# TensorE's order in a group pass: the sums over spans in two blocks behind up 7 and down 5, and up of chunk 0 ahead of routing

## The chip, the core and the metric

The kernel runs on one core of a Trainium2 chip. The core has TensorE (matmuls), VectorE (DVE), ScalarE (ACT), GpSimd (POOL) and SyncE (SP, which here starts DMAs), each with its own instruction stream; they meet only at semaphores. The metric is the time of one execution in microseconds (us), the median over several runs.

## What is computed

A block of a network over 16 sequences of 256 tokens with 128 features, in fp32: a selective-scan layer (a state-space recurrence with 16 states), and behind it a feed-forward layer with one shared expert and eight routed ones, of which each token takes two. Both are modulated by a small table of scales and shifts. Cut to what matters:

```python
h = _layernorm(x) * (1 + ca) + sa
xc, z = split(h @ W_in)
xs = silu(conv(xc) + conv_b)                     # 4 taps along time
x_dbl = xs @ W_x
delta = softplus(x_dbl[..., :1]); Bp = ...; Cp = ...
A_bar = exp(delta * A); B_bar = delta * Bp
h_t = A_bar_t * h_(t-1) + B_bar_t * x_t;  y_t = sum_n h_t * C_t
x = x + ga * (((y + D * xs) * silu(z)) @ W_out)
h = _layernorm(x) * (1 + cb) + sb
out = swiglu(h, shared) + sum over top 2 of 8 experts: weight * swiglu(h, expert)
x = x + gb * out
```

The kernel doesn't step through time. It multiplies by decays exp(a * sum of delta over a span), for spans that halve (128, 64, 32, 16) and for pairs of tokens within blocks of 16. The sums of delta over these spans are matmuls of constant 0/1 matrices with delta: these are the "sums over spans".

## The kernel before

The 4096 tokens are worked in eight groups of 512 (two sequences). The loop over groups is `body(g, prev, head)`, written once for each engine: body(0) outside a loop, body(1) to body(6) in a hardware loop, body(7) behind it. In a pass three pieces of work are woven together, each engine's order written out by hand:

- the head of group g+1 (`head`): layer norm, W_in (project_in), convolution, W_x (project_x), softplus, the sums over spans, the decays and factors;
- the middle of group g: factors turned (turn_factors), weighed and mixed (weigh, mix), W_out (project_out), residual, second norm, h2 turned (turn_h2);
- the tail of group g-1 (`prev`): routing logits and picks, and the shared expert in eight chunks c of its 938 hidden features. Each chunk has `gate(c)` and `up(c)`, three 512-column matmuls each (a weight's low part, high part, and the input's low part), a silu on ScalarE, a product on VectorE, a split into high and low parts (`ah`, `al`), and `down(c)`, which adds to one result bank. The numbers "up 7", "down 5" and "product 6" mean these chunks. Chunk 3 is the short one.

In the passes ("NARROW") all gates share PSUM bank 5 and all ups bank 6, so gate(c) waits until silu c-1 has read the bank, and up(c) until product c-1 has. The tail's result is copied by ScalarE (y_sb), turned by TensorE (turn_result), multiplied on VectorE into `gated`, and added to X on GpSimd.

The sums over spans (`sum_spans(g+1)`, line 722) wait for `delta_ready`, which VectorE gives with dl_upto (line 1290), and end with `spans_done`, for which VectorE's `level_exponents` (line 1293 and on) waits. They are five products with delta (ten matmul records of 2 or 4 columns: fp32 takes two passes) and one with dl_upto (two records, 64 columns). In VectorE's order stand make_delta (delta, dl_upto, dB), product 6, second_norm (nx_b, h2), product 7, level_exponents, pair_exponents, low_x, factors, gate_shared (gated), pairs_by_c, take_logits; then in the next body product 0, sum_pairs (wd, line 1341), product 1. GpSimd's pairs_by_b (pair, line 489) stands between pairs_by_c and sum_pairs.

`route(g-1)` is twelve matmuls of 8 columns that wait for xh and xl, the high and low parts of the tail's input; turn_x waits for nx_a, ScalarE's normalised input of the next head.

Behind the passes stands the wide part: the last group's shared expert and the routed experts' tiles, and then the final sum.

Of the kernel before, what the change touches and what calls it, by code (L numbers as in the profile page):

```python
# [39 lines left out]
GC = CH // G  # L40
# [73 lines left out]
def adaln_block(nc, a):  # L114
    ctx = ExitStack()
    with ctx:
        def sb(name, shape, dt=F32):
            return ctx.enter_context(nc.sbuf_tensor(name, shape, dt))

        def sem(name):  # L120
            return ctx.enter_context(nc.semaphore(name))
# [8 lines left out]
        M = {n: mats[:, i, :] for i, n in enumerate(CONST)}  # L130
# [43 lines left out]
        delta = sb("delta", [P, GC])  # L174
# [58 lines left out]
        PS = ctx.enter_context(nc.psum_tensor("PS", [P, 8, 512], F32))  # L233
# [4 lines left out]
        NARROW = {"gate": (5,), "up": (6,), "down": 7, "turn": 5}  # L238
# [6 lines left out]
        def bank(kind, where, c=0):  # L245
            b = where[kind]
            return PS[:, b if isinstance(b, int) else b[c % len(b)], :]

        def part_of(c):

            return c if c < SHORT else FC - 1 if c == SHORT else c - 1
# [21 lines left out]
        s = {n: sem("s_" + n) for n in names}  # L273
# [327 lines left out]
        def _(pe):  # L601
            def mm(out, lhsT, rhs, start=True, stop=True, **k):
                return nc.tensor.matmul(out, lhsT, rhs, start=start, stop=stop, **k)  # L603

            def turn(out, src):
                return nc.tensor.transpose(out, src, M["ident"])  # L606

            def high_part(out, buf, w0, rh, start):

                mm(out, w_lo[buf][:, w0:w0 + P], rh, start, False)  # L610
                mm(out, w_hi[buf][:, w0:w0 + P], rh, False, False)

            def low_part(out, buf, w0, rl, stop):

                return mm(out, w_hi[buf][:, w0:w0 + P], rl, False, stop)
# [15 lines left out]
            def up(buf, I, c, where):  # L631
                out = bank("up", where, c)
                if where is NARROW and c:
                    pe.wait_ge(s["prod_done"], I * FC + c)
                w0 = UP + part_of(c) * P
                high_part(out, buf, w0, xh[:], True)
                low_part(out, buf, w0, xl[:], True).then_inc(s["up_done"], 1)
# [6 lines left out]
            def down(buf, I, c, where):  # L644
                pe.wait_ge(s["ah_ready"], I * FC + c + 1)
                out, w0 = bank("down", where), DOWN + part_of(c) * P
                if c != SHORT:
                    high_part(out, buf, w0, ah[:, c % 3, :], c == 0)
                else:
                    mm(out, w_lo[buf][0:FL, w0:w0 + P], ah[0:FL, c % 3, :], False, False)  # L650
                if where is WIDE:
                    pe.wait_ge(s["al_ready"], I * FC + c + 1 - (FC - CUT) * (G - 1))
                elif c < CUT:
                    pe.wait_ge(s["al_ready"], I * CUT + c + 1)
                else:
                    pe.wait_ge(s["al_late"], I * (FC - CUT) + c - CUT + 1)
                if c != SHORT:
                    last = low_part(out, buf, w0, al[:, c % 3, :], c == FC - 1)
                else:
                    last = mm(out, w_hi[buf][0:HALF + FL, w0:w0 + P], ah[0:HALF + FL, c % 3, :], False, False)  # L660
                if c == FC - 1:
                    last.then_inc(s["y_bank_done"], 1)
                elif c < FC - 3:
                    last.then_inc(s["down_done"], 1)
# [49 lines left out]
            def gather_c(g):  # L714

                pe.wait_ge(s["cexp_ready"], g + 1)
                pe.wait_ge(s["xst_ready"], 2 * g + 2)
                for k in range(2):
                    mm(PS[:, 3 + k, :], M["upto16"], c_exp[:, 2 * k:2 * k + 2].rearrange("p j a n -> p (j a n)")
                       ).then_inc(s["cg_done"], 1)  # L720

            def sum_spans(g):

                pe.wait_ge(s["delta_ready"], g + 1)
                out = PS[:, 2, 256:256 + 4 * GC].rearrange("p (l j) -> p l j", l=4)
                mm(out[:, 0, 0::2], M["below7"], delta[:, 0::2])
                mm(out[:, 0, 1::2], M["above7"], delta[:, 1::2])
                for k, n in enumerate(("lvl6", "lvl5", "lvl4")):
                    mm(out[:, k + 1, :], M[n], delta[:])
                mm(PS[:, 2, 320:320 + GC * BLK], M["later16"], dl_upto[:].rearrange("p j a -> p (j a)")).then_inc(  # L730
                    s["spans_done"], 1)

# [39 lines left out]
            def turn_h2(g, more):  # L772
                pe.wait_ge(s["h2_ready"], g + 1)
                if more:
                    pe.wait_ge(s["sz_ready"], 2 * g + 4)
                for j in range(GC):
                    last = turn(PS[:, 0, j * P:(j + 1) * P], h2[:, 0, j, 0:P])
                last.then_inc(s["h2T_done"], 1)

            def route(g):  # L780
                pe.wait_ge(s["xh_ready"], g + 1)
                pe.wait_ge(s["xl_ready"], g + 1)
                for j in range(GC):
                    o = PS[:, 1, j * E:(j + 1) * E]
                    mm(o, xl[:, j * P:(j + 1) * P], gate_hi[:], True, False)
                    mm(o, xh[:, j * P:(j + 1) * P], gate_lo[:], False, False)
                    last = mm(o, xh[:, j * P:(j + 1) * P], gate_hi[:], False, True)
                last.then_inc(s["logits_done"], 1)
# [19 lines left out]
            project_x(0)  # L808
            turn_xs(0, True)
            sum_spans(0)  # L810
            gather_c(0)

            def body(g, prev, head):
                if prev:
                    route(g - 1)
                if head:
                    turn_x(g + 1, False, prev)
                if prev:
                    gate(0, g - 1, 0, NARROW)
                    up(0, g - 1, 0, NARROW)  # L820
                    gate(0, g - 1, 1, NARROW)
                    up(0, g - 1, 1, NARROW)
                turn_factors(g)
                if prev:
                    gate(0, g - 1, 2, NARROW)
                if head:
                    project_in(g + 1, 0, prev)
                weigh(g)
                if prev:
                    up(0, g - 1, 2, NARROW)  # L830
                    count_picks(g - 1, COUNTS)
                    up(0, g - 1, 3, NARROW)
                mix(g, 0)
                if prev:
                    gate(0, g - 1, 4, NARROW)
                if head:
                    project_in(g + 1, 1, prev)
                mix(g, 1)
                if prev:
                    gate(0, g - 1, 5, NARROW)  # L840
                if head:
                    project_in(g + 1, 2, prev)
                if prev:
                    down(0, g - 1, 0, NARROW)
                if head:
                    project_in(g + 1, 3, prev)
                if prev:
                    up(0, g - 1, 4, NARROW)
                    gate(0, g - 1, 6, NARROW)
                project_out(g, head)  # L850
                if prev:
                    gate(0, g - 1, 7, NARROW)
                    down(0, g - 1, 1, NARROW)
                    up(0, g - 1, 5, NARROW)
                if head:
                    project_x(g + 1)
                if prev:
                    down(0, g - 1, 2, NARROW)
                if head:
                    turn_xs(g + 1, False)  # L860
                if prev:
                    down(0, g - 1, 3, NARROW)
                    down(0, g - 1, 4, NARROW)
                    up(0, g - 1, 6, NARROW)
                if head:
                    sum_spans(g + 1)
                if prev:
                    up(0, g - 1, 7, NARROW)
                    down(0, g - 1, 5, NARROW)
                turn_h2(g, head)  # L870
                if head:
                    gather_c(g + 1)
                if prev:
                    down(0, g - 1, 6, NARROW)
                    down(0, g - 1, 7, NARROW)
                    turn_result(g - 1, NARROW)

            body(0, False, True)
            pe.wait_ge(s["split_done"], 1)
            apart(pe)  # L880
# [813 lines left out]
```

## Time and profile before

| | |
|---|---|
| Time, median of 3 runs | 783.69 us (783.38 to 783.82) |
| The profiled execution's own time | 781.73 us |
| Its span, first to last instruction | 779.9 us |
| TensorE busy | 669.7 us, 86% of the span |
| VectorE busy | 561.2 us, 72% |
| ScalarE busy | 431.6 us, 55% |
| GpSimd busy | 375.4 us, 48% |
| Mean granted TensorE clock | 0.928 of full speed |

The profile is of one execution. Its times count from the span's start. A timeline lists the instructions of one engine: start, duration, line, operation, out<-in, shape, how many were merged, and in brackets the idle time ahead of it and what ended that. Line 603 is the helper `mm` and 606 the helper `turn` of TensorE, 1248 the product, 961 the silu. Ends of matmuls are modelled: from the start of one to the start of the next is the surer price. A granted clock of 1.00 is 2.4 GHz, 0.50 is 1.2 GHz.

### The profile page before, as it was taken

To read this page: it belongs to the slowest core of one execution; us is meant where nothing else is said; L and a number is where in the kernel's file an instruction comes from. 1 tells how busy PE (TensorE), PEld (TensorE's weight loads), DVE (VectorE), ACT (ScalarE), POOL (GpSimd) and SP (SyncE) were. 2 spreads that over 40 slices of the span, in tenths; PEclk is the share of its full clock that TensorE was granted. 3 is DMA by queue.
4 is the path that set the end of the run, shared out by engine and by line. 5 is a ranking of instruction groups with operands and counts; after the bars stand their busy time and mean duration, and the time that the engine had idled before them with its cause. 6 is when DMAs were issued, how large, how long until landed. Compare 5 with 4: busy or idle time off the path is not lost.

```text
span 779.9 us, 12016 instructions
## 1 busy us (share of the span) xinstructions
PE 669.7 (86%) x3026; PEld 503.3 (65%) x3027; DVE 561.2 (72%) x1230; ACT 431.6 (55%) x822; POOL 375.4 (48%) x299
## 2 busy tenths in 40 slices
PE   4768989899899989897789998999999998999910
PEld 1546767677666766674557776777677776777700
DVE  4878969889797979985647665666666675766637
ACT  4457566675757656653445554555555565555600
POOL 1323654647384554636318291836154172922145
PEclk9598979999998989989799999999999999999965
DMA  8303000000000000010310322313103103110046
GB/s 257 90 1 96 28 27 19 10 30 24 27 27 27 27 12 28 14 34 22 116 49 6 128 65 82 92 41 116 39 17 116 41 4 116 43 34 21 27 139 194
DMA packets 41297, 44.55 MB, mean 57 GB/s; under 512 B 8052, under 2 KB 31976, under 8 KB 41280
## 3 DMA queue, kind: packets, MB, share of 16 engines
q1 hardware_dynamic: 36672, 35.88, 15.6%
q0 software_dynamic: 4608, 8.47, 3.3%
q8 instruction: 7, 0.11, 0.1%
q14 instruction: 10, 0.08, 0.0%
HBM read 31.61 MB, written 13.76 MB: 58 GB/s over the span
## 4 chain that ended last, share of the span: by engine, by line
PE 37%; DVE 27%; issue 16%; POOL 11%; DMA 3%; SPq 2%; ACT 2%; POOLq 1%; DVEq 1%; ACTq 0%
PE PS L603 33%; POOL w_lo L434 4%; PE PS L606 4%; DVE acc L1268 3%; POOL w_hi L429 3%; DVE al L1255 3%; DVE prod L1248 2%; SPq L306 2%; DMA xin<-sorted_dram 1%; POOL pair L489 1%; DVE yT L1358 1%; DVE wd L1341 1%; POOL result_dram L562 1%; DVE PS L1248 1%; POOL sorted_dram L499 1%
## 5 line engine op out<-in xcount | busy, mean ns | idle before, releaser
L961 ACT ACTIVATE sg<-PS 128x512 f32<-128x512 f32 x216 | 128.7, 596 | 150.1 <-PE PS L603 148.8
L603 PE MATMUL PS<-xh,w_lo 128*128 128x512 f32 x405 | 177.2, 438 | 15.8 <-issue 7.1
L1248 DVE TENSOR_TENSOR PS<-PS,sg 128x512 f32<-128x512 f32 (+1 forms) x160 | 111.3, 697 | 109.1 <-PE PS L603 98.3
L562 POOL DMA_INDIRECT result_dram<-y_rows,aux_d x80 | 78.0, 975 | 186.7 <-DVE y_rows L1620 156.1
L603 PE MATMUL PS<-xh,w_hi 128*128 128x512 f32 x405 | 162.9, 402 | 0.0
L603 PE MATMUL PS<-xl,w_hi 128*128 128x512 f32 x405 | 162.8, 402 | 0.0
L499 POOL DMA_INDIRECT sorted_dram<-h,slot x64 | 74.0, 1156 | 90.0 <-DVE slot L1455 64.1
L603 PEld LDWEIGHTS PS<-xh,w_lo 128*128 128x128 f32 x405 | 78.3, 193 | 48.8 <-DVE prod L1248 13.5
L1255 DVE TENSOR_TENSOR al<-PS,ah 128x512 fp32r<-128x512 f32 x140 | 95.5, 682 | 7.7 <-ACT ah L969 5.0
L603 PE MATMUL PS<-ah,w_lo 128*128 128x512 f32 x216 | 96.5, 447 | 3.8 <-ACT ah L969 3.8
L969 ACT CAST ah<-PS 128x512 fp32r<-128x512 f32 (+1 forms) x160 | 92.8, 580 | 8.5 <-DVE PS L1248 8.1
L603 PEld LDWEIGHTS PS<-xl,w_hi 128*128 128x128 f32 x405 | 78.7, 194 | 18.2
L603 PE MATMUL PS<-ah,w_hi 128*128 128x512 f32 x216 | 88.6, 410 | 0.8 <-DVE ah L1255 0.8
L603 PEld LDWEIGHTS PS<-xh,w_hi 128*128 128x128 f32 x405 | 78.9, 195 | 13.4 <-issue 1.4
L603 PE MATMUL PS<-al,w_hi 128*128 128x512 f32 x189 | 76.0, 402 | 2.3 <-POOL al L452 1.2
L603 PEld LDWEIGHTS PS<-ah,w_lo 128*128 128x128 f32 x216 | 41.2, 191 | 22.6 <-issue 11.2
L1248 DVE TENSOR_TENSOR prod<-PS,sg 128x512 f32<-128x512 f32 (+1 forms) x56 | 38.5, 688 | 20.1 <-PE PS L603 14.1
L603 PEld LDWEIGHTS PS<-ah,w_hi 128*128 128x128 f32 x216 | 41.6, 192 | 16.8 <-issue 8.0
L969 ACT CAST ah<-prod 128x512 fp32r<-128x512 f32 (+1 forms) x56 | 34.4, 615 | 32.5 <-DVE prod L1248 29.8
L452 POOL TENSOR_TENSOR al<-prod,ah 128x512 fp32r<-128x512 f32 x28 | 38.7, 1384 | 20.5 <-ACT ah L969 20.4
L434 POOL TENSOR_TENSOR w_lo<-stage,w_hi 128x3072 fp32r<-128x3072 f32 x7 | 47.9, 6838 | 0.6
L603 PEld LDWEIGHTS PS<-al,w_hi 128*128 128x128 f32 x189 | 36.2, 191 | 12.9 <-DVE al L1255 3.1
(223 smaller groups left out, 1114.9 us busy)
## 6 DMA issues: line engine op xcount, KB each, us to landing
stage<-in_w_gu SPq DMA_DIRECT2D x18, 448.0 KB
xin<-sorted_dram SPq DMA_DIRECT2D x20, 260.0 KB, 2.7
stage<-in_w_dn SPq DMA_DIRECT2D x9, 448.0 KB
tab<-mods_dram SPq DMA_DIRECT2D x8, 384.0 KB, 3.6
sorted_dram<-pad SPq DMA_DIRECT2D x8, 260.0 KB, 2.4
out<-X SPq DMA_DIRECT2D x4, 512.0 KB, 3.2
stage<-result_dram SPq DMA_DIRECT2D x3, 512.0 KB, 5.2
result_dram<-y_rows,aux_d POOLq DMA_INDIRECT x80, 2.2
```

Of the source, the lines that this page charges most:

```text
L429: V.tensor_tensor(w_hi[buf][:], stage[:], M["ones"][:, 0:1].to_broadcast([P, WC]), ALU.mult).then_inc(s["split_hi"], 1)
L434: V.tensor_tensor(w_lo[buf][:], stage[:], w_hi[buf][:].bitcast(F32), ALU.subtract).then_inc(s["split_done"], 1)
L452: V.tensor_tensor(al[:, c % 3, :], prod[:, c % 3, :], ah[:, c % 3, :].bitcast(F32), ALU.subtract).then_inc(s["al_late"], 1)
L499: pool.indirect_dma_start(out=sorted_dram, out_offset=bass.IndirectOffsetOnAxis(ap=slot[:, k, j:j + 1].bitcast(U32), axis=0), in_=h2[:, k, ...
L562: pool.indirect_dma_start(out=result_dram, out_offset=bass.IndirectOffsetOnAxis(ap=aux_d[:, r:r + 1].bitcast(U32), axis=0), in_=y_rows[:, ...
L603: return nc.tensor.matmul(out, lhsT, rhs, start=start, stop=stop, **k)
L606: return nc.tensor.transpose(out, src, M["ident"])
L961: A.activation(dst, src, ACT.Silu).then_inc(s["silu_done"], 1)
L969: A.copy(ah[0:n, c % 3, :], product_in(where, c)[0:n, :]).then_inc(s["ah_ready"], 1)
L1248: V.tensor_tensor(product_in(where, c)[0:n, :], bank("up", where, c)[0:n, :], sg[0:n, c % 3, :], ALU.mult).then_inc(s["prod_done"], 1)
L1255: V.tensor_tensor(dst, product_in(where, c)[0:n, :], ah[0:n, c % 3, :].bitcast(F32), ALU.subtract).then_inc(s["al_ready"], 1)
L1268: last = V.scalar_tensor_tensor(o, xcp[:, h, :, k:k + SEQ], cols[:, h, k:k + 1], o, ALU.mult, ALU.add)
```

## The change

TensorE's stream alone is changed, in three places. (1) `sum_spans` keeps the sums with below7, above7 and lvl6; the rest (lvl5, lvl4 and the one on dl_upto, with the increment of `spans_done`) is a new function, `sum_low_spans`. (2) In body, sum_spans(g+1) stands behind up 7 instead of ahead of it, and sum_low_spans(g+1) behind down 5. (3) up(0) of the tail stands ahead of route, behind waits for xh and xl, instead of behind gate(0).

```diff
@@ sum_spans
                 mm(out[:, 0, 1::2], M["above7"], delta[:, 1::2])
-                for k, n in enumerate(("lvl6", "lvl5", "lvl4")):
-                    mm(out[:, k + 1, :], M[n], delta[:])
+                mm(out[:, 1, :], M["lvl6"], delta[:])
+
+            def sum_low_spans(g):
+
+                out = PS[:, 2, 256:256 + 4 * GC].rearrange("p (l j) -> p l j", l=4)
+                for k, n in ((2, "lvl5"), (3, "lvl4")):
+                    mm(out[:, k, :], M[n], delta[:])
                 mm(PS[:, 2, 320:320 + GC * BLK], M["later16"], dl_upto[:].rearrange("p j a -> p (j a)")).then_inc(
                     s["spans_done"], 1)
@@ before the loop
             sum_spans(0)
+            sum_low_spans(0)
             gather_c(0)
@@ body
                 if prev:
+                    pe.wait_ge(s["xh_ready"], g)
+                    pe.wait_ge(s["xl_ready"], g)
+                    up(0, g - 1, 0, NARROW)
                     route(g - 1)
                 if head:
                     turn_x(g + 1, False, prev)
                 if prev:
                     gate(0, g - 1, 0, NARROW)
-                    up(0, g - 1, 0, NARROW)
                     gate(0, g - 1, 1, NARROW)
                     up(0, g - 1, 1, NARROW)
...
                     up(0, g - 1, 6, NARROW)
+                if prev:
+                    up(0, g - 1, 7, NARROW)
                 if head:
                     sum_spans(g + 1)
                 if prev:
-                    up(0, g - 1, 7, NARROW)
                     down(0, g - 1, 5, NARROW)
+                if head:
+                    sum_low_spans(g + 1)
                 turn_h2(g, head)
```

## Rows read from the trace of the kernel before

**Rows 1.** The page, part 4: the chain's shares of the span by engine.
```profile
PE 37%; DVE 27%; issue 16%; POOL 11%; DMA 3%; SPq 2%; ACT 2%; POOLq 1%; DVEq 1%; ACTq 0%
```

**Rows 2.** Chain that ended last, in pass 5: start us, us, what, count.
```profile
277.62 5.12 PE PS L603 x18
...
287.44 0.59 ACT y_sb L973
...
288.94 0.70 DVE gated L1462
...
292.32 1.30 POOL pair L489
```

**Rows 3.** TensorE's timeline, pass 5: start, us, line, operation, [idle before].
```profile
277.62 1.92 PE L603 MATMUL PS<-delta,mats 128*128 128x2 f32 x10 [1.12 <-DVE dl_upto L1290]
...
279.83 0.78 PE L603 MATMUL PS<-xh,w_lo 128*128 128x512 f32 x1
...
281.26 0.63 PE L603 MATMUL PS<-ah,w_lo 128*128 128x512 f32 x1
...
282.54 1.05 PE L606 MATMUL PS<-mats,h 128*128 128x128 f32 x4
...
285.46 0.79 PE L603 MATMUL PS<-ah,w_lo 128*128 128x512 f32 x1
```

**Rows 4.** VectorE's timeline, pass 5.
```profile
277.49 1.30 DVE L1292 TENSOR_TENSOR dB<-delta,dbc 128x64 f32<-128x64 f32 x1
279.07 0.69 DVE L1248 TENSOR_TENSOR prod<-PS,sg 128x512 f32<-128x512 f32 x1 [0.28 <-DVE dB L1292]
...
282.16 0.41 DVE L1297 TENSOR_TENSOR lev<-PS,a_neg 128x256 f32<-128x256 f32 x1
...
286.67 0.75 DVE L1324 TENSOR_TENSOR pq<-lev_b,small 128x64 f32<-128x64 f32 x3
```

**Rows 5.** Windows: us, busy by engine, granted clock, DMA share, GB/s; pass 5.
```profile
279.00:280.00 1.00, 1.00 (x6) 1.00 (x7) 0.93 (x2) 0.14 (x1) 0.00 (x0) 0.50 0.00 0
285.00:286.00 1.00, 1.00 (x4) 0.52 (x3) 0.96 (x6) 0.65 (x2) 0.00 (x0) 1.00 0.00 0
```

**Rows 6.** Pass 6: TensorE's timeline, VectorE's, and one window.
```profile
322.12 1.28 PE L603 MATMUL PS<-delta,mats 128*128 128x2 f32 x10 [1.12 <-DVE dl_upto L1290]
323.26 0.41 PE L603 MATMUL PS<-dl_upto,mats 128*128 128x64 f32 x2
324.31 0.50 PE L603 MATMUL PS<-xh,w_lo 128*128 128x512 f32 x1 [0.64 <-DVE prod L1248]
...
329.17 0.40 PE L603 MATMUL PS<-al,w_hi 128*128 128x512 f32 x1
...
331.18 0.68 DVE L1462 TENSOR_TENSOR gated<-PS,tab_g 128x512 f32<-128x512 f32 x1
...
325.00:326.00 1.00, 1.00 (x7) 0.65 (x6) 0.68 (x1) 0.96 (x2) 0.94 (x1) 1.00 0.00 0
```

**Rows 7.** Pass 1: VectorE's timeline, then TensorE's.
```profile
101.42 0.69 DVE L1248 TENSOR_TENSOR prod<-PS,sg 128x512 f32<-128x512 f32 x1 [0.28 <-DVE dB L1292]
...
103.63 0.77 PE L603 MATMUL PS<-xh,w_lo 128*128 128x512 f32 x1
```

**Rows 8.** Tile dl_upto: duration ns min/median/max of its weight loads.
```profile
L603 PEld LDWEIGHTS PS<-dl_upto,mats x16: 192/333/333, 29.3 to 323.3; 128*128 128x128 f32 x16
```

**Rows 9.** Around up 0 and gate 1, pass 5: TensorE, then VectorE, then ScalarE.
```profile
290.33 0.63 PE L606 MATMUL PS<-mats,nx_a 128*128 128x128 f32 x4 [0.21 <-ACT nx_a L1053]
...
291.49 0.40 PE L603 MATMUL PS<-xh,w_lo 128*128 128x512 f32 x1
...
292.34 0.50 PE L603 MATMUL PS<-xh,w_lo 128*128 128x512 f32 x1
...
292.45 0.69 DVE L1248 TENSOR_TENSOR prod<-PS,sg 128x512 f32<-128x512 f32 x1 [1.18 <-PE PS L603]
...
291.68 0.60 ACT L961 ACTIVATE sg<-PS 128x512 f32<-128x512 f32 x1 [0.29 <-PE PS L603]
```

## The prediction

> **What bounds the kernel now.** I read the page first, and of it the chain of work that ended last: it lies 37% on TensorE and 27% on VectorE [rows 1]. A share over 780 us mixes stages, so next comes the chain in order of time inside one group pass. The changed order acts in body(g) for g = 1 to 7, of which passes 1 to 6 also hold the head of the next group, and so the sums over spans. They repeat every 44.5 us; I work on pass 5 (the one whose end lies near 287 us) and hold it against passes 1 and 6. There the chain is short to tell: from the sums over spans at 277.62 TensorE runs without a stop, over up 7, down 5, the turn of h2, the gathering of C, down 6 and down 7, to the copy of the result at 287.44. Behind it stand ScalarE's copy y_sb, the turn of the result, VectorE's gated at 288.94, GpSimd's pair product up to 293.62, and then the reduction to wd, from which VectorE's routing of the tail goes on [rows 2]. So from 277.62 to 287.4 TensorE is the bound of the pass, and its orders there count one for one.
>
> Then I ask what starts that stretch. In TensorE's rows up 6 ends about 276.5, the engine stands 1.12 us until dl_upto is written, the 12 records of the sums start at 277.62, and up 7 at 279.83 [rows 3]. In VectorE's rows dB runs from 277.49 to 278.79 and product 6, which up 7 must wait for (one PSUM bank serves all "up" chunks of a narrow pass), from 279.07 to 279.76 [rows 4]. Up 7 thus starts 0.07 us behind product 6: the sums lie in a hole that up 7 could not have used. That is the observation on which the forecast rests.
>
> **The change part by part.**
>
> *Sums over spans, moved behind up 7 and down 5.* The work is the same: 12 records in all. At the old place they fill the hole 277.6 to 279.8; at the new one the hole stays empty, and they stand inside the stretch where TensorE is the bound. Their price, start to next start: 279.83 - 277.62 = 2.21 us at half speed [rows 3]; at full speed 323.26 - 322.12 = 1.14 for the ten narrow ones and 0.41 for the two on dl_upto, 1.55 us [rows 6].
>
> What they gain: up 7 may start when product 6 ends. In pass 5 that is 279.76 against 279.83, so nothing; in pass 6 up 7 already stands behind product 6 (0.64 us of idle, released by it) [rows 6]. Only pass 1 has a gain: its product 6 ends at 102.11, up 7 starts at 103.63 [rows 7], 1.5 us, of one pass.
>
> What could hide them: a wait of TensorE behind up 7. Down 5 at 281.26, the turn of h2 at 282.54 and down 6 at 285.46 all start with no idle ahead of them [rows 3], and the chain stays on TensorE up to y_sb [rows 2]. There is none.
>
> Who waits for the later sums: level_exponents on VectorE, queued behind product 7, with the pair exponents, low_x, the factors and gated behind it. The sums would be done at 279.83 + 1.43 (up 7) + 1.28 (down 5) + 2.21 = 284.75. From the start of the exponents at 282.16 to the end of the factors at 287.42 VectorE takes 5.26 us, of which some is a wait for xh; from 284.75 that gives 290.0 [rows 4]. Gated needs the result's turn, so it moves from 288.94 [rows 2] to about 291. So VectorE stays ahead by 0.8 to 1 us and adds nothing at half speed. ScalarE (level and pair exponentials) follows VectorE's exponents and comes before y_sb in its queue; y_sb waits for down 7, some 2 us later than now, so this adds nothing either. No DMA, no queue of SP or GpSimd is passed; GpSimd only waits for gated, later.
>
> *The clock.* In pass 5 the granted clock is 0.50 (1.2 of 2.4 GHz) in 279:280, and 1.00 again in 285:286 [rows 5]. Before the fall the engine had stood 1.12 us and then run only narrow sums. In pass 6 it stayed at 1.00 behind the same idle time [rows 6]. Over all passes the weight loads for dl_upto took 192 ns at least and 333 ns in the median [rows 8], so at least half of the 16 ran slowly. After the change TensorE stands from 276.5 to 279.8, 3.3 us instead of 1.1, and the narrow sums then lie between wide matmuls. I expect the low level in all six passes, and for at least as long as now. Price of this, with pass 5's own durations: up 7 1.43, sums 2.21, down 5 1.28, turn and gathering 282.54 to 285.46, 2.92, downs 6 and 7 285.46 to about 287.4, 1.95 [rows 2, 3]; 9.8 us from up 7's start to the last down, against 7.6 now. In pass 6, all at full speed, it is 324.31 to 329.57, 5.3 us now [rows 6], so there up to +4.5. If the downs too run slowly (six at 0.43, from 281.26 to 282.54 for three) the stretch has 10.4 us.
>
> The sum: for passes 1 to 5 the added time lies between the sums' full-speed price 1.55 and their half-speed price 2.21. I take 2.0, since the granted clock has usually come back for the last downs and pass 1 gives some of it back. For pass 6, which loses the full clock, I take 4.0 of the 4.5. 5 x 2.0 + 4.0 = 14.0 us.
>
> *Up of chunk 0 ahead of routing.* Three wide matmuls, 292.34 less 291.49, 0.85 us, move ahead of the 12 routing matmuls. Nobody waits for them sooner: product 0 starts at 292.45 behind up 0, but the reduction behind it is bound by GpSimd's pair product, which ends at 293.62 and starts when it is done with gated [rows 2, 9]. The hole that takes them is small: the turn of x starts at 290.33 when nx_a is there, behind 0.21 us of idle. So the turn, gate 0 and silu 0 come about 0.45 us later (0.6 to 0.7 of up 0 less the idle), silu 0 at 292.1 for 0.60; product 0 no longer waits for up 0 at 292.45 but for silu 0 near 292.75, and ends at 293.45 instead of 293.14, still ahead of 293.62. The logits come some 0.7 us later, and their copy has an idle stretch of 1.18 us behind it on VectorE [rows 9]. Cost 0; bounds from the hole's 0.2 us gained and 0.3 us lost (product 0's shift, if the pair product came earlier), times 7: -1.4 to +2.1. In pass 7, without a turn of x, gate 0 and the rest shift by the same and end in the same wait.
>
> *Setup.* sum_spans(0) and sum_low_spans(0) stand together, and body(0) has nothing between them: no change. Two waits on xh and xl are repeated in front of route: they are met already when route comes, nothing.
>
> **How a rule of the Trainium skill bears on this.** The row shows 0.11 to 0.13 us for each narrow sum at full speed and weight loads of 192 or 333 ns for dl_upto [rows 6, 8]. The Trainium skill, page "TensorE: Matmul & The Clock Gate", section "Step-by-step: what each phase is for", says that the next tile's weights load while this tile's matmul runs. By it the first sum of each block would load behind the wide matmul ahead of it, which it could not do at the old place, behind a wait. No row of before has sums right behind wide matmuls.
>
> **The rivals.**
>
> A. *The first load of each block hides behind the wide matmul ahead of it.* For: weight loads overlap wide matmuls all through the page. Against: it takes one load per block only, the rest stand between narrow matmuls. Price: 2 x 0.33 us in each of six passes, 4 us less: 793.7. That is the result that the skill's sentence above would give.
>
> B. *The low level holds to the end of the stretch.* 10.4 - 7.6 = 2.8 for five passes, 5.1 for pass 6: +19.1, 802.8. For: the wide work that went before the clock's return in pass 5 comes later. Against: in pass 5 it came back although the stretch was not all wide matmuls.
>
> C. *The clock does not fall at all, or less than now.* Full speed gives 5.3 + 1.55 = 6.8 us from product 6, against 7.6 in pass 5: five passes gain 0.8, pass 6 loses about 1.3, in all -2.7, and with falls in some passes about 0: 783.7. For: pass 6. Against: three times the idle time ahead of the stretch.
>
> D. *Faster: the sums find a wait.* If TensorE had an idle stretch between up 7 and down 7 as long as the sums (1.55 us), they would be free there, and up 7 would start with product 6 in each pass as it could in pass 1. It decides from the point where the idle exceeds 1.55 us; pass 1 then gives 1.5 us and up 0's early start its 0.2 us a pass: -2.9, 780.8. Against: no idle of that stretch in the chain.
>
> E. *VectorE becomes the bound through the late sums.* In pass 6, at full speed, gated starts at 331.18 now with no idle ahead of it, straight behind the factors [rows 6]: there VectorE is level with TensorE already. If VectorE's stretch of 5.26 us grew by more than the 0.8 us of slack, each further 0.5 us would cost 3: 800.7.
>
> **How the numbers follow.** The profiled execution ran 781.73 us with a span of 779.9; the median of the three runs is 783.69, 2.0 above. Both should shift alike: span 793.9, median 783.69 + 14.0 = 797.7. Chances: forecast 0.60, A 0.13, B 0.12, C 0.07, D 0.03, E 0.05. The range reaches down past A with the lower bound of up 0 and full-speed price for the sums (5 x 1.55 + 1.3 = 9.0, less what A hides in some passes): 790; up to B and a little of up 0's upper bound: 803.5. A measurement of this kernel can tell about 0.2%, 1.6 us, from no change. Faster: 0.03 (D). Same: 0.06 (most of C). Slower: the rest, 0.91.
>
> **What the profile after would show.** Right: up 7 starts within 0.1 us of product 6's end and is preceded by about 3.3 us of idle; the sums stand behind it in two blocks with no idle ahead of them; the last down ends about 9.4 to 9.8 us behind product 6; the period of a pass is 46.5 to 47 us instead of 44.5; granted clock 0.50 through most of that stretch in all six passes; VectorE waits longer ahead of the exponents and less ahead of gated; wd still follows the pair product at once. Wrong: idle of TensorE between up 7 and the turn of h2 that grew (the sums hidden, D), a granted clock of 1.00 there (C), gated released by VectorE's own factors (E), or wd preceded by product 0 instead of GpSimd (then up 0 has a price).

## The result, and the profile after

The changed kernel takes 806.83 us (median of four runs, 802.37 to 809.67), the kernel before 783.76 beside it: 1.0266 times the time, 95% interval 1.0221 to 1.0311. The change is slower, as forecast; but 23 us slower instead of 14, and above the range's end of 803.5. Medians and ranges, here and below, are over all runs; ratios and intervals are estimated without the four runs that lie more than 1.5% above the fastest of their kernel (792.5 us of up 0 alone, 817.7 of the sums alone, 783.2 and 785.7 of the kernel before with 4 and 2 matmuls added), so that a ratio can differ a little from the quotient of the medians, which is 1.029 here. The profiled execution took 805.35 us, its span is 803.6, against 779.9.

The page of the changed kernel: busy time by engine, then the chain's shares by engine.

```profile
PE 677.1 (84%) x3026; PEld 507.6 (63%) x3027; DVE 562.1 (70%) x1230; ACT 431.2 (54%) x822; POOL 374.8 (47%) x299
...
PE 37%; DVE 25%; issue 17%; POOL 10%; DMA 3%; ACT 3%; SPq 2%; POOLq 1%; DVEq 1%; ACTq 0%
```

TensorE runs the same 3026 records, 7 us more of busy time, and its share of the chain is the same 37% as in [rows 1]. Nothing on the page shows where 24 us went; it takes the pass.

TensorE's timeline of the changed kernel, pass 5 (start, us, line, operation, out<-in, shape, count, idle before). It answers to [rows 3].

```profile
292.93 0.80 PE L603 MATMUL PS<-xh,w_lo 128*128 128x512 f32 x1 [3.31 <-DVE prod L1259]
...
294.37 1.27 PE L603 MATMUL PS<-delta,mats 128*128 128x2 f32 x6
295.51 0.77 PE L603 MATMUL PS<-ah,w_lo 128*128 128x512 f32 x1
...
296.93 0.85 PE L603 MATMUL PS<-delta,mats 128*128 128x4 f32 x4
297.64 0.67 PE L603 MATMUL PS<-dl_upto,mats 128*128 128x64 f32 x2
298.10 1.06 PE L606 MATMUL PS<-mats,h 128*128 128x128 f32 x4
298.95 3.46 PE L603 MATMUL PS<-c_exp,mats 128*128 128x512 f32 x4
301.59 1.06 PE L603 MATMUL PS<-ah,w_lo 128*128 128x512 f32 x1
```

VectorE's timeline of the same pass, answering to [rows 4] and to gated in [rows 2].

```profile
292.18 0.69 DVE L1259 TENSOR_TENSOR prod<-PS,sg 128x512 f32<-128x512 f32 x1 [0.28 <-DVE dB L1303]
...
298.35 0.42 DVE L1308 TENSOR_TENSOR lev<-PS,a_neg 128x256 f32<-128x256 f32 x1 [2.98 <-PE PS L603]
...
305.33 0.69 DVE L1473 TENSOR_TENSOR gated<-PS,tab_g 128x512 f32<-128x512 f32 x1 [2.34 <-PE PS L606]
...
309.13 0.69 DVE L1259 TENSOR_TENSOR prod<-PS,sg 128x512 f32<-128x512 f32 x1 [1.46 <-ACT sg L972]
310.03 1.22 DVE L1352 TENSOR_REDUCE wd<-pair 128x64 f32<-128x1024 f32 x1 [0.20 <-POOL pair L489]
```

The order of events is the one that the prediction told. TensorE stands 3.31 us for product 6; up 7 starts 0.06 us behind product 6's end (292.87); the sums follow in two blocks with no idle ahead of them; VectorE waits 2.98 us for them, but still also 2.34 us for the result's turn, so it isn't the bound. The period of a pass, from gated to gated, is 47.69 to 47.80 us; the prediction had 46.5 to 47. Product 0 now waits for silu 0 and has ended (309.82) when the pair product lets wd start at 310.03.

What is larger than told is the stretch from product 6's end to the copy of the result, y_sb. Everything outside it is unchanged: from gated to product 6's end the passes take 35.30 to 35.34 us, against 35.30 to 35.52 before. The view for such a stretch is the one of windows (columns: length, busy us and count of TensorE, its weight loads, VectorE, ScalarE, GpSimd, then granted clock, DMA share, GB/s). First the kernel before, passes 1 to 6:

```profile
102.11:110.60 8.49, 8.46 (x28) 6.20 (x28) 5.94 (x15) 4.15 (x8) 3.03 (x2) 0.69 0.00 0
147.62:154.54 6.92, 6.83 (x20) 4.42 (x20) 6.39 (x18) 4.15 (x9) 3.03 (x2) 0.75 0.00 0
191.34:198.28 6.94, 6.85 (x20) 4.14 (x20) 6.41 (x17) 4.05 (x8) 3.02 (x2) 0.75 0.00 0
235.11:242.93 7.82, 7.79 (x21) 4.96 (x20) 6.57 (x17) 4.15 (x8) 3.03 (x2) 0.65 0.00 0
279.76:287.44 7.68, 7.65 (x22) 4.94 (x21) 6.56 (x17) 4.15 (x8) 3.03 (x2) 0.67 0.00 0
324.26:329.61 5.35, 5.26 (x20) 3.25 (x20) 4.82 (x10) 4.05 (x9) 3.04 (x2) 1.00 0.00 0
```

Then the changed kernel, passes 1, 3 and 6 and the sum of the six:

```profile
102.11:112.90 10.79, 10.70 (x32) 7.71 (x32) 6.61 (x18) 4.15 (x8) 3.02 (x2) 0.59 0.00 0
...
197.41:208.32 10.91, 10.82 (x32) 7.74 (x32) 6.59 (x17) 4.15 (x9) 3.03 (x2) 0.58 0.00 0
...
340.64:351.63 10.99, 10.90 (x32) 7.75 (x32) 6.60 (x18) 4.15 (x8) 3.01 (x2) 0.58 0.00 0
sum 65.45, PE 64.90 PEld 46.42 DVE 39.59 ACT 24.90 POOL 18.14; mean PE 10.82 PEld 7.74 DVE 6.60 ACT 4.15 POOL 3.02
```

The six stretches add up to 43.20 us before and 65.45 after: 22.25 of the span's 23.7 us lie here. The granted clock differs as much as the length. A mean of 0.58 over 10.91 us is (1 - 0.58) x 2 x 10.91 = 9.2 us at 1.2 GHz of 2.4; before it was 5.1 us in pass 5 (0.67 of 7.68) and none in pass 6. Now all six passes are alike. Windows around the low level of pass 5 show when it begins and ends, first in the kernel before, then in the changed one.

```profile
277.10:278.00 0.90, 0.38 (x4) 0.38 (x4) 0.90 (x2) 0.66 (x2) 0.90 (x2) 1.00 0.00 0
278.10:284.80 6.70, 6.70 (x22) 5.28 (x22) 5.36 (x9) 3.31 (x7) 3.64 (x3) 0.50 0.00 0
285.00:287.40 2.40, 2.40 (x9) 1.32 (x7) 2.37 (x11) 0.65 (x2) 0.00 (x0) 1.00 0.00 0
```

```profile
290.90:291.80 0.90, 0.00 (x0) 0.00 (x0) 0.90 (x1) 0.00 (x0) 0.90 (x1) 1.00 0.00 0
291.90:302.10 10.20, 9.17 (x27) 6.80 (x27) 6.39 (x15) 4.15 (x8) 3.03 (x2) 0.50 0.00 0
302.20:303.80 1.60, 1.60 (x7) 0.94 (x5) 0.80 (x4) 0.00 (x0) 0.00 (x0) 1.00 0.00 0
```

The clock fell at about 291.9, while TensorE stood, 1.0 us ahead of product 6's end, and stayed low for 10.2 us; before, the low level lasted 6.8 us. In all six passes of the changed kernel it lasts 10.2 us; in those of the kernel before, 6.8 us in three, 3.4 us in two, and in pass 6 it doesn't fall in the stretch. Since each pass repeats the one before it, with the fall at nearly the same place (1.0 to 1.4 us ahead of product 6's end), the six are not six independent cases. The remaining 1.5 us is the net of smaller shifts behind the passes; the largest is +3.3 in the routed tiles, told below.

### The profile page after: what moved, and what is told of

It is laid out like the page before. It is cut to its first block, busy times and chain, and to the rows that moved or that the text cites. A ratio compares the mean times of both kernels' runs of the same rounds, so it can differ in the third digit from the quotient of the medians.

```text
span 803.6 us, 12023 instructions
## 1 busy us (share of the span) xinstructions
PE 677.1 (84%) x3026; PEld 507.6 (63%) x3027; DVE 562.1 (70%) x1230; ACT 431.2 (54%) x822; POOL 374.8 (47%) x299
## 4 chain that ended last, share of the span: by engine, by line
PE 37%; DVE 25%; issue 17%; POOL 10%; DMA 3%; ACT 3%; SPq 2%; POOLq 1%; DVEq 1%; ACTq 0%
PE PS L603 33%; PE PS L606 4%; POOL w_lo L434 3%; POOL w_hi L429 3%; DVE al L1266 2%; DVE acc L1279 2%; DVE prod L1259 2%; SPq L306 1%; DMA xin<-sorted_dram 1%; POOL pair L489 1%; POOL result_dram L562 1%; DVE yT L1369 1%; DVE wd L1352 1%; DVE dB L1303 1%; DMA result_dram<-y_rows,aux_d 1%
## 5 line engine op out<-in xcount | busy, mean ns | idle before, releaser
L603 PE MATMUL PS<-ah,w_lo 128*128 128x512 f32 x216 | 99.5, 461 | 3.8 <-ACT ah L980 3.8
L452 POOL TENSOR_TENSOR al<-prod,ah 128x512 fp32r<-128x512 f32 x28 | 38.7, 1383 | 19.1 <-ACT ah L980 19.0
```

Of the source, the lines that this page charges most:

```text
L452: V.tensor_tensor(al[:, c % 3, :], prod[:, c % 3, :], ah[:, c % 3, :].bitcast(F32), ALU.subtract).then_inc(s["al_late"], 1)
```

## The experiments

"Narrow" matmuls are those of 2 to 64 columns, "wide" ones have 512. All medians are taken beside runs of the kernel before on the same chip (783.2, 784.3, 784.0 and 782.2 us in the four groups). "Stretch" is always that from product 6's end to y_sb.

**Up of chunk 0 alone.**

```diff
                 if prev:
+                    pe.wait_ge(s["xh_ready"], g)
+                    pe.wait_ge(s["xl_ready"], g)
+                    up(0, g - 1, 0, NARROW)
                     route(g - 1)
...
                     gate(0, g - 1, 0, NARROW)
-                    up(0, g - 1, 0, NARROW)
```

> The kernel before with only the third part: up of chunk 0 ahead of routing. Theory (the cost is all in the moved sums; product 0 is covered by GpSimd's pair product): 783.7 us, within 1.5 us, and 35.3 us from gated to the end of product 6 in a pass, as in both kernels. Rival (up 0's place has a price, 0.3 us a pass, or more through the clock): 786 us or above, and gated to product 6 longer than 35.3.

Measured: 785.97 us (five runs, 777.3 to 792.5), ratio 1.0057, interval 1.0021 to 1.0093. From gated to product 6's end 35.31 to 35.35 us in the profiled execution, which itself was the fastest run, 777.31. The same kernel again, with more runs:

> The kernel before with only up of chunk 0 ahead of routing, a second time with more runs, since the first gave 777.3 to 792.5 us, scattered on both sides of the kernel before. Theory (no price in a pass; where the low clock falls in the passes differs from run to run): single runs again on both sides of 783.7, the median within 3 us of it, and 35.3 us from gated to the end of product 6. Rival (a steady price): all runs above 784, and a longer time from gated to product 6.

Measured: 784.44 us (twelve runs, 780.8 to 792.4), ratio 1.0032, interval 1.0002 to 1.0063. So there is a small price of 0.3 to 0.6%, not shown to be steady: runs lie on both sides. Of the rival's two signs one is absent, for not all runs are above 784, and the other is there in part: in this profiled execution the time from gated to product 6's end is longer in two passes of five. The windows that end with product 6 of passes 3 and 4:

```profile
156.00:191.28 35.28, 31.45 (x172) 23.96 (x170) 31.04 (x78) 23.10 (x41) 21.93 (x19) 1.00 0.09 30
198.20:235.52 37.32, 34.45 (x172) 26.84 (x170) 30.88 (x79) 23.14 (x41) 21.93 (x19) 0.89 0.08 28
```

At full clock the pass part takes 35.28 us, so up 0's place costs nothing there. Where the clock was low in it, it takes 37.32, twice among the five. Each of the two followed a stretch at full clock (5.35 us), so here the clock took in one place what it had given in the one before. That is no rule: in the profiled execution of the first run the stretch of pass 3 was at full clock too (5.33 us), and the time up to product 6 of pass 4 was 35.34 us.

**The sums alone.** The changed kernel with up 0 put back.

```diff
-                    up(0, g - 1, 0, NARROW)
                     route(g - 1)
...
                     gate(0, g - 1, 0, NARROW)
+                    up(0, g - 1, 0, NARROW)
```

> The kernel before with only the sums moved (block 1 behind up 7, block 2 behind down 5), up of chunk 0 left where it was. Theory: the whole loss, 804 to 809 us, passes of about 47.8 us, 10.8 to 11.0 us from the end of product 6 to the copy of the result. Rival (the two parts add up, or need each other): clearly under 802 us.

Measured: 809.68 us (four runs, 805.3 to 817.7; 806.23 is the median without the highest), ratio 1.0373, interval 1.0306 to 1.0441; stretches of 10.65 to 10.94 us, 65.09 in all. The whole loss is in the moved sums.

**The changed kernel, with the standstill filled.**

```diff
+            def fill(I, n):
+
+                pe.wait_ge(s["silu_done"], I * FC + FC)
+                for k in range(n):
+                    mm(PS[:, 5, :], w_hi[0][:, 0:P], xh[:])
...
                     up(0, g - 1, 6, NARROW)
                 if prev:
+                    fill(g - 1, 12)
                     up(0, g - 1, 7, NARROW)
```

> The changed kernel with 12 more wide matmuls in each pass, on a PSUM bank that nobody reads then, between up 6 and up 7, where TensorE stands 3.3 us for product 6. Work is only added. Theory (of the 3.7 us a pass some 2 are the clock, which falls because TensorE stands still, and the rest the sums at their full-speed price of 1.55): the granted clock stays at 1.00 in the stretch, 6.8 to 7.2 us from product 6 to the copy of the result instead of 10.9, total 783.7 plus or minus 3. Rival (the low clock comes from the narrow sums between the wide matmuls, not from the standstill): low level in the stretch as before, 10 us or more, total 804 or above.

Measured: 782.72 us, ratio 0.9992, interval 0.9976 to 1.0007. Wide matmuls are added, 72 in the six passes and 12 in body(7), which has the tail too (TensorE has 3110 records instead of 3026), and 24 us are gone. The window of pass 5 and the sum of the six:

```profile
280.14:286.74 6.60, 6.50 (x32) 4.66 (x32) 5.51 (x14) 4.17 (x9) 3.04 (x2) 1.00 0.00 0
...
sum 39.55, PE 39.00 PEld 28.01 DVE 33.01 ACT 24.97 POOL 18.21; mean PE 6.50 PEld 4.67 DVE 5.50 ACT 4.16 POOL 3.03
```

The clock is at 1.00 in all six, over the same sums at the same place: without a standstill ahead of them they do not take it down. 6.59 us on average is a little less than the 6.8 that I had expected at least. The sums at their new place cost 6.60 - 5.35 = 1.25 us at full clock, with pass 6 of the kernel before as the other end. The rest of the 10.91, 4.3 us, is the clock. Part of what is saved here comes back elsewhere: from gated to product 6's end four of five passes take 36.2 to 37.4 us instead of 35.3.

**Standstill short, sums at the new place too.** Sums moved as in the change, up of chunk 0 as in the kernel before, and a copy of all twelve done first at the old place.

```diff
                     up(0, g - 1, 6, NARROW)
+                if prev and head:
+                    copy_sums(g + 1)     # the six products, into columns 384 on of bank 2
                 if prev:
                     up(0, g - 1, 7, NARROW)
```

> The sums moved as in the change (up of chunk 0 as before), and a copy of all 12 sums done a first time at the old place ahead of up 7, into columns that nobody reads. The standstill is then as short as in the kernel before, and the sums stand at the new place too. If the long low clock comes from the longer standstill alone: the sums add only their own price, 1.55 to 2.2 us a pass, so 9 to 9.5 us from product 6 to the copy of the result and 793 to 797 us in all. If narrow matmuls count as little better than standstill for the clock: the low level lasts 10.2 us in each pass as in the changed kernel, 10.8 us for the stretch, 804 us or above.

Measured: 809.83 us, ratio 1.0344, interval 1.0312 to 1.0377. TensorE's timeline, pass 5:

```profile
292.63 1.38 PE L603 MATMUL PS<-delta,mats 128*128 128x2 f32 x10 [1.12 <-DVE dl_upto L1311]
293.87 0.67 PE L603 MATMUL PS<-dl_upto,mats 128*128 128x64 f32 x2
294.83 0.80 PE L603 MATMUL PS<-xh,w_lo 128*128 128x512 f32 x1 [0.28 <-DVE prod L1269]
...
296.27 1.27 PE L603 MATMUL PS<-delta,mats 128*128 128x2 f32 x6
```

The idle ahead of up 7 is close to that of the kernel before, 1.12 us and then 0.28 (there 1.12 and then, in pass 5, none), and still the stretches take 10.77 to 10.95 us from pass 2 on, and 11.71 in pass 1. That it is TensorE's idle time of 3.3 us which makes the low level last is refuted.

**Standstill long, no sums at all.** The sums are left out of passes 1 to 6; VectorE is released by down 5 and reads an earlier group's sums. Only the passes are read; the whole took 788.01 us, in its single run.

```diff
-                if head:
+                if head and not prev:
                     sum_spans(g + 1)
                 if prev:
                     up(0, g - 1, 7, NARROW)
-                    down(0, g - 1, 5, NARROW)
+                    last = down(0, g - 1, 5, NARROW)
+                if prev and head:
+                    last.then_inc(s["spans_done"], 1)
```

> The kernel before with the sums over spans left out of passes 1 to 6 (VectorE is released by down 5 and reads the sums of an earlier group, so the output is not the reference's, and the routing and the number of tiles may differ: only the passes are to be read). TensorE stands 3.3 us as in the changed kernel, and no sums follow. If the standstill takes the clock down for the whole stretch: 8.5 to 8.8 us from product 6 to the copy of the result (10.9 less the sums at 2.2). If the clock falls no more than in the kernel before: 7.2 us on average, as there.

Windows of the six stretches, pass 5 and the sum; ahead of it the row of up 7.

```profile
285.55 0.79 PE L603 MATMUL PS<-xh,w_lo 128*128 128x512 f32 x1 [3.31 <-DVE prod L1251]
```

```profile
285.49:293.20 7.71, 7.62 (x20) 4.88 (x20) 6.60 (x18) 4.15 (x8) 3.03 (x2) 0.66 0.00 0
...
sum 43.44, PE 42.88 PEld 26.80 DVE 38.95 ACT 24.69 POOL 18.20; mean PE 7.15 PEld 4.47 DVE 6.49 ACT 4.12 POOL 3.03
```

43.44 us in six passes, against 43.20 in the kernel before, though TensorE stood 3.08 to 3.31 us each time. The clock did fall in all six, for 3.4 us in four and 6.8 us in two. A standstill of 3.3 us thus goes with a fall, but without the sums behind it the low level is no longer than it was.

**The same, with wide matmuls for the sums.** Three wide matmuls at the place of each block.

```diff
                 if prev:
                     up(0, g - 1, 7, NARROW)
+                if prev and head:
+                    fill(g - 1, 3)
+                if prev:
                     last = down(0, g - 1, 5, NARROW)
                 if prev and head:
-                    last.then_inc(s["spans_done"], 1)
+                    fill(g - 1, 3).then_inc(s["spans_done"], 1)
```

> As the run without sums in passes 1 to 6 (so again the output is not the reference's, and only the passes are to be read), but where the changed kernel has its two blocks of narrow sums, behind up 7 and behind down 5, there stand three wide matmuls each, six in all, which take as long as the sums or a little more (6 x 0.43 = 2.6 us at half speed, 1.4 at full). Theory (it is the narrow matmuls in the stretch that keep the clock at the low level for 10.2 us): the low level lasts 3.4 or 6.8 us as in the run without sums, and the stretch from product 6 to the copy takes 7.2 + 1.4 to 2.6, so 8.6 to 9.3 us on average. Rival (any added work of this length there costs the same 3.7 us): 10.9 us.

```profile
285.36:293.61 8.25, 8.15 (x26) 5.59 (x26) 5.48 (x14) 4.16 (x9) 3.04 (x2) 0.79 0.00 0
...
sum 51.13, PE 50.56 PEld 34.88 DVE 33.32 ACT 24.93 POOL 18.24; mean PE 8.43 PEld 5.81 DVE 5.55 ACT 4.16 POOL 3.04
```

8.52 us a pass, 1.28 more than without and just under the 8.6 that I had expected at least: the six wide matmuls cost about their full-speed price (6 x 0.23 = 1.4). The whole took 793.34 us in its single run. Twelve narrow ones at the same place, with 1.25 us of full-speed price, cost 10.91 - 7.24 = 3.67. At 0.79 of 8.25 us the clock was low for 3.5 us, with the narrow ones for 9.2.

Part of this difference is where the fall comes. In four passes of the swap it comes later than in the changed kernel. Only in passes 1 and 4 does it come as early, 1.0 us ahead of product 6's end. The stretch of pass 4, and its low level:

```profile
238.85:248.19 9.34, 9.24 (x26) 6.41 (x26) 5.71 (x15) 4.16 (x9) 3.04 (x2) 0.69 0.00 0
237.90:244.60 6.70, 5.70 (x14) 4.43 (x15) 2.85 (x5) 2.21 (x4) 3.04 (x2) 0.50 0.00 0
244.80:248.10 3.30, 3.30 (x13) 1.78 (x11) 3.27 (x10) 1.94 (x4) 0.00 (x0) 1.00 0.00 0
```

Like for like, the low level lasts 6.8 us with wide matmuls and 10.2 with narrow ones, and the stretch takes 9.3 us against 10.9: so 1.6 of the mean difference of 2.4 us are what the narrow matmuls do to the level once it has fallen, and the rest comes from the later falls.

**Half of the move, and one block.** First, only the low block (lvl5, lvl4, dl_upto) moves behind down 5. Then, in another kernel, all sums stand behind up 7.

```diff
@@ half of the move, against the kernel before
                 if prev:
                     up(0, g - 1, 7, NARROW)
                     down(0, g - 1, 5, NARROW)
+                if head:
+                    sum_low_spans(g + 1)
@@ one block, against the kernel before
-                if head:
-                    sum_spans(g + 1)
                 if prev:
                     up(0, g - 1, 7, NARROW)
+                if head:
+                    sum_spans(g + 1)
+                if prev:
                     down(0, g - 1, 5, NARROW)
```

> Half of the move: the first block of sums stays ahead of up 7, only the low block (six records) goes behind down 5; up of chunk 0 as before. If each sum costs its own price in TensorE's stretch: about 0.9 to 1.1 us a pass, 6 us, and with some more of the low clock up to 12: 789 to 796 us. If the loss comes from the long standstill only: near 784 to 787 us, for the first block still stands in the hole.

> The sums over spans whole, in one block, behind up 7 and ahead of down 5; up of chunk 0 as before. Tells whether the split into two blocks bears any of the loss. Theory (narrow matmuls in the stretch lengthen the low level, wherever they stand): 10.4 to 11.0 us for the stretch, passes of about 47.8 us, 803 to 812 us. Rival (the second block, right ahead of the turn of h2, does the harm): clearly less, 797 us or under.

Measured: half of the move 806.01 us, ratio 1.0296 (1.0243 to 1.0349), stretches 10.29 to 10.49 us; one block 803.25 us, ratio 1.0255 (1.0220 to 1.0291), stretches 10.96 or 10.97 in all six. The half I missed: I had given it at most 796. Its stretches grew by 19.2 us in all, and in four of five passes the time from gated to product 6's end by 0.6 us each. Its pass 5:

```profile
292.54:302.96 10.42, 10.32 (x26) 6.89 (x26) 6.60 (x18) 4.15 (x9) 3.03 (x2) 0.54 0.00 0
```

Six narrow records instead of twelve, half the work moved, and nearly the whole loss, at a clock of 0.54. Here too the low level lasts 10.2 us in each pass. The clock's part of the loss is a step, not a sum over records; where between none and six records the step lies was not tried. The split into two blocks plays no part.

**The kernel before, with its holes filled.** Wide matmuls ahead of the sums and between the sums and up 7.

```diff
+                if prev and head:
+                    fill(g - 1, 4)       # 5 in the second kernel
                 if head:
                     sum_spans(g + 1)
+                if prev and head:
+                    fill(g - 1, 2)       # 3 in the second kernel
                 if prev:
                     up(0, g - 1, 7, NARROW)
```

> The kernel before with 4 more wide matmuls in each pass in TensorE's 1.1 us of idle ahead of the sums, and 2 between the sums and up 7. Theory (the standstill takes the clock down, and the stretch behind product 6 is TensorE's): the clock stays at 1.00 there in most passes, the stretch takes 5.3 us as pass 6 of before did, instead of 6.9 to 8.5, total 772 to 777 us. Rival (the sums themselves are what the low clock comes from, or the added matmuls push up 7 back): 783 us or above.

> The kernel before with 5 wide matmuls added ahead of the sums and 3 between the sums and up 7 (the run with 4 and 2 gave 776.5 us). Theory (more wide work in TensorE's holes keeps the full clock in more passes, at under 0.1 us of delay each at full speed): 771 to 776 us. Rival (the hole is full already, and what is added delays up 7, at twice the price where the clock has fallen): 777 to 782 us.

Measured: 4 and 2: 776.52 us (ten runs, 771.5 to 785.7), ratio 0.9892 (0.9858 to 0.9927), with four of the six stretches at full clock and two of 6.9 us with 3.4 us at the low level; 5 and 3: 776.62 us (775.3 to 778.5), ratio 0.9910 (0.9884 to 0.9937), just above what I had expected of it. Both beat both kernels, the kernel before by 1%. Six stretches of the second, pass 5 and the sum:

```profile
273.84:279.19 5.35, 5.32 (x21) 3.25 (x20) 4.82 (x11) 4.06 (x8) 3.05 (x2) 1.00 0.00 0
...
sum 32.95, PE 32.73 PEld 20.42 DVE 29.54 ACT 24.34 POOL 18.28; mean PE 5.46 PEld 3.40 DVE 4.92 ACT 4.06 POOL 3.05
```

10.3 us less than the 43.20 of the kernel before, of which some 2.5 us come back from gated to product 6's end (35.5 to 36.1 us a pass instead of 35.3).

## Why the prediction was right and wrong

**Right.** The stretch in which TensorE bounds the pass: 22.25 of 23.7 us lie in it. That up 7 wins nothing by the sums' going, since product 6 ends at the same time; even in pass 1, where I saw 1.5 us to win, up 7 did start at once and the stretch still grew from 8.49 to 10.79. That no wait hides the sums, that VectorE keeps some slack (I said 0.8 to 1 us and a shorter wait ahead of gated; it waited 2.34 us for the turn, 1.52 before), and that product 0 stays ahead of the pair product. Low level in all six passes came true as well, which refutes rival C. Rival D, the one with the gain, had nothing for it, and rival E is refuted by gated's releaser.

**Wrong: the step on the clock.** I summed 2.0 us for passes 1 to 5, "since the granted clock has usually come back for the last downs". That is the step that failed: it priced the sums alone and put the longer low level at nothing. The passes grew by 2.3, 3.9, 4.0, 3.1 and 3.3 us, mean 3.3. Pass 6, put at 4.0, grew by 5.6. The low level lasted 10.2 us instead of 6.8, and the clock came back only in the first of the six last matmuls, at about 302.1 in pass 5, where I had it back for the downs and partly for the gathering. Split with the filled kernel: full-speed work 6.59 against 5.35, so +1.25; lost to the clock 10.91 - 6.59 = 4.3 against 7.20 - 5.35 = 1.85, so +2.5. I had priced the sums too high (1.55 to 2.2) and the clock too low, and the two errors did not cancel. Rival B, at a chance of 0.12, came nearest, with 19.1 us and 802.8; its 10.4 us for the stretch is 0.5 short: the turn and gathering, taken with part of it at full speed, took 3.49 us (298.10 to 301.59), not 2.92, and down 5 and the sums 0.24 us more, while the last downs took 0.33 us less than at half speed throughout.

**Left open there: why the clock stays low.** The prediction named two things together, a standstill of 3.3 us instead of 1.1 and the narrow sums between wide matmuls, and against rival C it argued from the standstill alone. The runs separate them. A standstill as long with no sums behind it leaves the stretch as it was (7.24 us), a short one with the sums behind it gives the full loss (10.9). Filling the standstill with wide matmuls did keep the clock up, so wide work ahead matters for whether it falls; but what holds it low once it has fallen is the narrow matmuls between the wide ones. The swap for wide matmuls of equal length shows it: 1.28 us instead of 3.67 on average, and 9.3 us instead of 10.9 for the stretch where the fall comes equally early. The kernels without sums there and with the swap were each seen in one execution; the full or nearly full loss was seen in five kernels, with 10.2 us of low level in all of their 30 passes.

**Rival A and the rule.** The rule of the Trainium skill, page "TensorE: Matmul & The Clock Gate", section "Step-by-step: what each phase is for", on loading the next weights under the running matmul, is not contradicted: at full clock the sums cost 1.25 us behind wide matmuls and 1.55 ahead of up 7, 0.3 us less. It is worth under 2 us over six passes, against 15 for the clock, so rival A's 793.7 is refuted by the size of what it left out.

**Up of chunk 0.** Forecast 0, bounds -1.4 to +2.1 us. Within a pass at full clock it is 0; over all runs the kernel with it alone is 0.3 to 0.6% slower, some 2.5 to 4.5 us, above my upper bound of 2.1. That this comes from where the low clock falls is seen in one execution and is not proven for the others. Beside the moved sums no addition is seen: 806.8 with it, and 809.7 without, or 806.2 without that kernel's highest run.

**Open.** The changed kernel took 385.5 us from the last gated to the end, the kernel before 382.2, though nothing in the routed tiles was changed. The waits of TensorE on the tiles' loads, kernel before and then changed kernel (us in total, times, longest):

```profile
PE PS L606 <- DMA xin<-sorted_dram: 3.8, 4, 1.3
```

```profile
PE PS L606 <- DMA xin<-sorted_dram: 7.1, 4, 1.9
```

That is the 3.3 us, but why the four loads came later was not tested; the kernel with one block has 382.9 there. Open too is why the runs of the changed kernel scatter over 7 us, and which condition exactly ends the low level.

## What to carry to other kernels

When work moves from a hole into a stretch where TensorE is the bound, its own time can be the smaller part of the price (here 1.25 of 3.7 us a pass); look at the granted clock of that stretch, pass by pass, before summing durations. Small matmuls should stand where the engine would be idle anyway, and not between wide ones just behind a wait, where the clock has fallen. Where the profile shows a fall behind a hole, wide matmuls that nobody reads, put into the hole, are a cheap test, and here gave 1%.

## What was not expected of the hardware

- Six narrow matmul records (2 to 64 columns) behind down 5 cost nearly as much as twelve (10.41 against 10.91 us for the stretch on average, 7.20 before): the low level lasted 10.2 us in both, and 3.4 or 6.8 us where no sums stood there.
- TensorE busy without a gap is no guard: in the changed kernel it is busy 10.87 of 10.97 us in the stretch of pass 5, at a mean clock of 0.58.
- A kernel with 84 added matmuls of 512 columns ran 24 us faster than without them, and one with 48 added ran 7 us faster than the kernel before.
- Low clock that is avoided in one place can partly return in another: 36.2 to 37.4 us instead of 35.3 in four of five passes of the changed kernel with the standstill filled.
